# Rounding the attention's outputs in its own steps, and joining the output projection to them

## The reference

```
x = x + xattn(layernorm(x), ctx)        # cross attention and own attention, fp8 weights and activations
x = x + sparse(layernorm(x))            # top-6 sparse attention
x = x + ternary_ffn(layernorm(x))       # ternary weights, 512 -> 2048 -> 512

def xattn(h, cond):
    ln_out = ln(h)
    q, k, v, qx = [fp8_linear(ln_out, w) for w in (wq, wk, wv, wqx)]     # q, qx: 16 heads of 128, k, v: 8
    core = gqa(ln(q), ln(k), v)                                          # within 64 tokens
    kx, vx = split(cond @ w_kv_x.T); kx = ln(kx)
    xout = gqa(ln(qx), kx, vx)                                           # over 1601 context tokens
    cat  = concatenate([core, xout], axis=-1)                            # 4096 features
    catq = fp8(bfloat16(clip(cat / proj_smooth, -448, 448)))
    return (catq @ wproj.T) * (proj_in_scale * proj_w_scale)
```

## Time and profile before

| | |
|---|---|
| three runs | 2127.19, 2126.93, 2124.67 us; median 2126.93 |
| the profiled execution | 2127.17 us, its span 2125.8 us |
| busy in the span | PE 1947.5 (92%), PEld 1641.5 (77%), DVE 1159.1 (55%), ACT 939.0 (44%), POOL 686.4 (32%) |

### The profile page before, as it was taken

How to read it: one execution, slowest core, us unless ns; L and a number is a source line. 1 busy time by engine, 2 the same in 40 slices (tenths; PEclk the granted TensorE clock), 3 DMA queues, 4 the chain that set the end, 5 groups by cost and what they waited for, 6 DMA issues and landing times. The chain is left out here.

```text
span 2125.8 us, 30938 instructions
## 1 busy us (share of the span) xinstructions
PE 1947.5 (92%) x10316; PEld 1641.5 (77%) x10316; DVE 1159.1 (55%) x2883; ACT 939.0 (44%) x1771; POOL 686.4 (32%) x734
## 2 busy tenths in 40 slices
PE   3899999999999999999999999999999994858769
PEld 3678888788888888888888888888888883642457
DVE  6565455445554554455446545554555443968743
ACT  4554344445544553354435534444544334518221
POOL 3224543322233332333333333343333322411310
PEclk9999999999999999999999999999999996989869
DMA  5775343435453543354445444443444225530020
GB/s 188 201 235 175 110 155 119 147 104 153 143 180 114 165 141 120 105 164 141 137 127 177 153 128 135 143 158 111 149 146 149 84 62 186 176 101 2 2 79 20
DMA packets 228588, 280.91 MB, mean 132 GB/s; under 512 B 63752, under 2 KB 134024, under 8 KB 228432
## 3 DMA queue, kind: packets, MB, share of 16 engines
q1 hardware_dynamic: 217936, 278.09, 41.6%
q10 hardware_dynamic: 8448, 0.43, 0.2%
q0 software_dynamic: 2048, 0.43, 0.1%
HBM read 239.10 MB, written 39.22 MB: 131 GB/s over the span
## 5 line engine op out<-in xcount | busy, mean ns | idle before, releaser
L496 PE MATMUL kx_ps<-ctxT_hi,wk_hi 128*128 128x400 f32 (+1 forms) x1024 | 366.4, 358 | 16.1 <-DVE ctxT_lo L295 14.9
L498 PE MATMUL kx_ps<-ctxT_lo,wk_hi 128*128 128x400 f32 (+1 forms) x1024 | 355.9, 348 | 0.0
L579 PE MATMUL u_ps<-ctxN_hi,pt_hi 128*128 128x512 f32 (+1 forms) x832 | 342.8, 412 | 13.5 <-DVE pt_lo L799 13.5
L500 PE MATMUL kx_ps<-ctxT_hi,wk_lo 128*128 128x400 f32 (+1 forms) x1024 | 355.2, 347 | 0.0
L580 PE MATMUL u_ps<-ctxN_lo,pt_hi 128*128 128x512 f32 (+1 forms) x832 | 331.9, 399 | 0.0
L581 PE MATMUL u_ps<-ctxN_hi,pt_lo 128*128 128x512 f32 (+1 forms) x832 | 330.2, 397 | 0.0
L799 DVE TENSOR_TENSOR pt_lo<-t_ps,pt_hi 128x512 fp32r<-128x512 f32 (+1 forms) x256 | 144.5, 587 | 277.1 <-ACT pt_hi L1039 277.1
L1008 ACT ACTIVATE kx_hi<-kx_ps 128x400 fp32r<-128x400 f32 (+1 forms) x256 | 129.3, 505 | 346.2 <-PE kx_ps L500 342.8
L726 DVE TENSOR_TENSOR kx_lo<-kx_ps,kx_hi 128x400 fp32r<-128x400 f32 (+1 forms) x256 | 147.0, 574 | 219.8 <-ACT sq L1010 219.6
L1039 ACT ACTIVATE pt_hi<-t_ps 128x512 fp32r<-128x512 f32 (+1 forms) x256 | 125.3, 523 | 286.2 <-PE t_ps L564 286.2
L781 DVE CUSTOM_DVE_ANT_0 prob<-sc_ps,rstd_bc 128x400 f32<-128x400 f32 (+2 forms) x256 | 136.4, 570 | 146.3 <-PE sc_ps L552 146.3
(11 more groups left out here) (247 smaller groups left out, 3647.6 us busy)
## 6 DMA issues: line engine op xcount, KB each, us to landing
rstd_bc<-scratch_rstd SPq DMA_DIRECT2D x64, 804.0 KB, 5.9
stage<-in_ctx_t SPq DMA_DIRECT2D x96, 267.0 KB, 4.6
stage<-in_ctx_n SPq DMA_DIRECT2D x96, 256.0 KB, 6.2
wk_hi<-scratch_wk_s SPq DMA_DIRECT2D x56, 256.0 KB, 3.2
wk_lo<-scratch_wk_s SPq DMA_DIRECT2D x56, 256.0 KB, 3.7
wv_hi<-scratch_wv_s SPq DMA_DIRECT2D x56, 256.0 KB, 4.9
wv_lo<-scratch_wv_s SPq DMA_DIRECT2D x56, 256.0 KB, 5.2
scratch_own_rows<-out_sb SPq DMA_DIRECT2D x32, 256.0 KB, 3.1
```

Of the source, the lines that this page charges most:

```text
L496: PE.matmul(kx_ps[:, j % 2, 0:w], wk_hi[:, g % 2, i, :], ctxT_hi[:, i, c0:c0 + w], start=(i == 0), stop=False)
L498: PE.matmul(kx_ps[:, j % 2, 0:w], wk_hi[:, g % 2, i, :], ctxT_lo[:, i, c0:c0 + w], start=False, stop=False)
L500: mm = PE.matmul(kx_ps[:, j % 2, 0:w], wk_lo[:, g % 2, i, :], ctxT_hi[:, i, c0:c0 + w], start=False, stop=(i == C - 1))
L579: PE.matmul(u_ps[:], pt_hi[0:w, t % 2, cols], ctxN_hi[0:w, y, :], start=(y == 0), stop=False)
```

## The change

- **Rounding.** In odd steps ACT's new `scale_outputs` scales a pair's outputs (four activations 128x64, two 128x128) and takes Abs (128x512), between `prob_high(n + 1, 1)` and `keys_high(n + 3, 3)`. In even steps DVE's new `round_outputs` does the four rounding operations, 512 wide, for the pair before, between `softmax_bias(n + 1)` and `keys_low(n + 3, 0)`. SP stores a pair in three DMAs, in even steps, where there were four over both steps. `cat` then holds `catq`.
- **Projection.** `project_out` goes; a class `Projection` stands in its place. Its first round is computed by PE in step 62 and its second in step 63, eight matmuls in each of four places; six rounds follow the last step. Rounds go in the order 0, 1, 4, 5, 2, 6, 3, 7, the last two token tile by token tile, with `acc_done` after each tile. The low parts of the weight are DVE's, `catq` is loaded ready, and no barrier stands ahead.
- **Norms.** `x2` and both norms are made tile by tile (`TileNorm`), in DVE's list of `attend`. POOL then waits for the last products and clears the semaphores, 119 now, ahead of the one barrier. The sparse attention's small weights are loaded in SP's list of `attend` (`Tail.load`, 13 DMAs).
- **Linear stage.** ACT makes all three high parts in item 0; DVE's low parts go in the sets `((0,), (1, 2, 3), (), ())`.
- Smaller: two semaphores of `softmax_bias` become one; the reciprocal of the smoothing is taken ahead of the steps; SBUF is laid out anew.

```diff
@@ tensor, attention @@
+                if n >= N - 2:
+                    PE.wait_ge(kx_split, 4 * N)
+                    proj.products(n - N + 2, 0, acc[0])
                 if v:
                     output(n)
...
                     keys(n + 3, 1)
+                if n >= N - 2:
+                    proj.products(n - N + 2, 1, acc[1])
                 if k:
                     keys(n + 3, 2)
+                if n >= N - 2:
+                    PE.wait_ge(scaled, 4 * N)
+                    proj.products(n - N + 2, 2, acc[2])
...
                     keys(n + 3, 3)
+                if n >= N - 2:
+                    proj.products(n - N + 2, 3, acc[3])
+            for k in range(2, 6):
+                for t in range(4):
+                    proj.products(k, t, acc[t])
+            PE.wait_ge(proj.cat_in[1], 16 * 4)
+            PE.wait_ge(proj.low_done, 8)
+            for t in range(4):
+                proj.products(6, t, acc[t])
+                proj.products(7, t, acc[t])
@@ vector @@
+            def round_outputs(u):
+                V.wait_ge(o_sized, u + 1)
+                V.tensor_scalar(o_y[:], o_y[:], 448.0, -448.0, ALU.min, ALU.max).then_inc(o_clipped, 1)
+                V.tensor_scalar(o_grid[:], o_grid[:], 1.5 * 2.0 ** 14, 448.0 * 2.0 ** 20, ALU.max, ALU.min).then_inc(o_stepped, 1)
+                V.wait_ge(o_clipped, u + 1)
+                V.wait_ge(o_stepped, u + 1)
+                V.tensor_tensor(o_res[:], o_y[:], o_grid[:], ALU.add).then_inc(o_lifted, 1)
+                V.wait_ge(o_lifted, u + 1)
+                after(V, o_stored, 48 * u)
+                V.tensor_tensor(o_cat[:], o_res[:], o_grid[:], ALU.subtract).then_inc(o_rounded, 1)
...
-                    for c in ((0,), (1,), (2, 3), ())[t]:
+                    for c in ((0,), (1, 2, 3), (), ())[t]:
                         weights_low(n + 1, c)
...
+                if v and not odd and u > 0:
+                    round_outputs(u - 1)
                 refill(3)
                 if k:
                     keys_low(n + 3, 0)
...
+                if N - 3 <= n < N - 1:
+                    proj.low(n - N + 3)
+            round_outputs(N // 2 - 1)
+            for k in range(2, 8):
+                proj.low(k)
...
+            residual(0)
+            for t in range(4):
+                middle(t)
+                if t < 3:
+                    residual(t + 1)
+                tail.norm2.vector_apply(t, tail.xln, tail.y)
@@ scalar @@
+            def scale_outputs(u):
+                g, head = u % G_, 16 + 4 * (u % (G_ // 2))
+                A.wait_ge(o_moved, 2 * u + 2)
+                A.wait_ge(own_moved, u + 1)
...
+                for h in range(4):
+                    part = slice(64 * (h % 2), 64 * (h % 2) + 64)
+                    A.activation(o_y[:, h // 2, part], o_res[:, h // 2, part], ACTF.Copy,
+                                 scale=recip_o[:, head + h:head + h + 1])
...
+                A.activation(o_grid[:], o_y[:], ACTF.Abs, scale=2.0 ** 20).then_inc(o_sized, 1)
...
-                if n + 1 < NB and t < 3:
-                    weights_high(n + 1, t)
+                if n + 1 < NB and t == 0:
+                    for c in range(3):
+                        weights_high(n + 1, c)
...
                     prob_high(n + 1, 1)
+                if v and odd:
+                    scale_outputs(u)
                 refill(6)
                 if k:
                     keys_high(n + 3, 3)
                 refill(7)
+                if N - 3 <= n < N - 1:
+                    proj.high(n - N + 3)
...
+            for k in range(2, 8):
+                proj.high(k)
@@ gpsimd @@
+            tail.norm1.gpsimd(0)
+            for t in range(4):
+                tail.norm2.gpsimd(t)
+                if t < 3:
+                    tail.norm1.gpsimd(t + 1)
+            G.wait_ge(proj.acc_done, 4)
+            G.wait_ge(tail.d_in, 16 * 11)
+            G.wait_ge(proj.high_done, 8)
+            core.clear_stage()
@@ sync @@
+                if n == N - 3:
+                    SP.wait_ge(kx_done, 4 * N)
...
+                    for k in range(2):
+                        proj.load_weights(k)
+                        proj.load_heads(k)
+                if n == N - 1:
+                    proj.load_weights(2)
...
+                if n > 0 and not odd:
+                    store_outputs(u - 1)
...
+            proj.load_weights(3)
+            store_outputs(N // 2 - 1)
+            proj.load_heads(2)
+            proj.load_heads(3)
+            SP.wait_ge(o_moved, N)
+            tail.load()
+            for k in range(4, 8):
+                proj.load_weights(k)
+                proj.load_heads(k)
```

More of the change, by code:

```diff
@@ new lines, with __init__, place, load_weights @@
+class Projection:
+    ORDER = (0, 1, 4, 5, 2, 6, 3, 7)
+    def __init__(self, core, o_stored):
+        self.c, self.o_stored = core, o_stored
+        sem = core.sem
+        self.cat_in, self.w_in = [sem("cat_in0"), sem("cat_in1")], [sem("wp_in0"), sem("wp_in1")]
+        self.high_done, self.low_done = sem("wp_high"), sem("wp_low")
+        self.part_done, self.acc_done = sem("proj_part"), sem("proj_acc")
+    def place(self, stack):
+        core = self.c
+        self.w_raw = core.sb(stack, "wp_raw", [P, 2, 4, 512])
+        self.catq = core.sb(stack, "catq", [P, 2, 4, 512], F32R)
+        self.w_hi = core.sb(stack, "wp_hi", [P, 2, 4, 512], F32R)
+        self.w_lo = core.sb(stack, "wp_lo", [P, 2, 4, 512], F32R)
+    def load_weights(self, k):
+        SP, b = self.c.SP, self.ORDER[k]
+        after(SP, self.low_done, k - 1)
+        SP.dma_start(self.w_raw[:, k % 2, :, :],
+                     self.c.dram["wprojT"][512 * b:512 * b + 512, :].rearrange("(f d) o -> d f o", d=P)
+                     ).then_inc(self.w_in[k % 2], 16)
+    def load_heads(self, k):
+        SP, b = self.c.SP, self.ORDER[k]
+        SP.wait_ge(self.o_stored, 48 * (26 + 2 * b if b < 4 else 25 + b))
+        after(SP, self.part_done, k - 1)
+        SP.dma_start(self.catq[:, k % 2, :, :].bitcast(F32),
+                     self.c.dram["cat"][4 * b:4 * b + 4, :, :].rearrange("f d s -> d f s")).then_inc(self.cat_in[k % 2], 16)
+    def high(self, k):
+        A = self.c.ACT
+        A.wait_ge(self.w_in[k % 2], 16 * (k // 2 + 1))
+        after(A, self.part_done, k - 1)
+        A.activation(self.w_hi[:, k % 2, :, :], self.w_raw[:, k % 2, :, :], ACTF.Copy).then_inc(self.high_done, 1)
+    def low(self, k):
+        V = self.c.DVE
+        V.wait_ge(self.high_done, k + 1)
+        V.tensor_tensor(self.w_lo[:, k % 2, :, :], self.w_raw[:, k % 2, :, :], self.w_hi[:, k % 2, :, :].bitcast(F32),
+                        ALU.subtract).then_inc(self.low_done, 1)
+    def products(self, k, t, bank):
+        PE = self.c.PE
+        if t == 0:
+            PE.wait_ge(self.cat_in[k % 2], 16 * (k // 2 + 1))
+            PE.wait_ge(self.low_done, k + 1)
+        for f in range(4):
+            PE.matmul(bank, self.catq[:, k % 2, f, t * P:(t + 1) * P], self.w_hi[:, k % 2, f, :],
+                      start=(k == 0 and f == 0), stop=False)
+            mm = PE.matmul(bank, self.catq[:, k % 2, f, t * P:(t + 1) * P], self.w_lo[:, k % 2, f, :],
+                           start=False, stop=(k == 7 and f == 3))
+        if k == 7:
+            mm.then_inc(self.acc_done, 1)
+        elif t == 3:
+            mm.then_inc(self.part_done, 1)
@@ L1994, in gpsimd @@
         def gpsimd():
-            norm.gpsimd(4)
+            norm.gpsimd(2)
             G.wait_ge(x_split, 2)
```

301 lines of the change are left out of this document (141 added, 160 removed).

## The result

The changed kernel takes 2090.22 us in the median of 4 runs (2086.96 to 2092.85), the kernel before beside it 2125.80 (2124.49 to 2127.19): a ratio of **0.9832**, 95% interval 0.9815 to 0.9849. That is 35.6 us less, where 45.3 were forecast (2082, range 2068 to 2104). The profiled execution took 2089.24 us, its span 2087.9.

What follows compares the result with a forecast made beforehand. PE was taken to bound the steps (busy 706.5 of 715 us), other engines the projection. Gains of 40.3 + 6 − 1 = 45.3 us off 2127.2 gave 2082, its own range 2072 to 2092, eight in ten 2068 to 2104.

Steps and rivals of the forecast that it cites:

- Part 1: Linear stage: PE's stalls cost 14.1 us, of which a replay with the new order leaves 8.0; gain 6.
- Part 2: Steps: rounding takes ACT 1.95 and DVE 2.0 us, hidden under PE with about 1 us slack; +1 taken overall.
- bound of −5: Steps: the lower bound on their cost, 5 us gained if the freed queue loads the context earlier.
- Parts 3 and 4: Last two steps and after: products end 5.8 us later, then PE stands 6.5 us instead of 25.8 before round 2.
- Part 5: Projection's six rounds after the steps: one wait of 5.2 us before rounds 6 and 7, end at 1844.2, 39.3 earlier.
- rival C: Projection: 13 transfers ahead on SP's list make round 4's weight and catq about 14 us late; 2096, chance 0.12.
- Part 6: Norms and clears: y_d 7.6 us after the products, clears 8.7, barrier 0.4; PE starts at 1860.4, gain 40.3.
- A: Linear stage: block 4's high parts come early enough and the waits vanish, 14 us instead of 6; about 2074, chance 0.13.
- B: Steps: PE notices the rounding at batch changes (13.7 us) and beside POOL's long operations (12.6); 2108, chance 0.12.
- D: Last two steps: products of rounds 0 and 1 stand in series instead of interleaving, 6 us lost; 2088, chance 0.03.
- E: Steps: the rounding lies wholly on PE's path, 122 us on top of −45; 2204, chance 0.05.
- the 6 us of waits between 83 and 130: Linear stage: a sign that the forecast is right, PE's waits there being 6 us in sum.

Runs made afterwards that it cites:

- stores late: The kernel before, with only the stores of the attention's outputs moved to the end of each step on SP's list: 2122.43 us beside 2124.05, ratio 0.9987.
- No rounding: The changed kernel with its new rounding work in the steps shrunk to one small ACT instruction and one DVE copy: steps 1579.03 us (one trace).

## Why the prediction was right, and where it was wrong

- **Part 1, the linear stage**: forecast 6, measured 6.6, and 2.8 to 5.8 in the other traces with the new order, so that 6 is at the upper end. The mechanism is right: block 4's three low parts still came behind the rounding. The replay put its wait at 4.2 (3.26 in the trace) and block 8's at 1.7 (0.68). Block 6's was not in it; it is 0.69 in this trace and up to 3.67 in others.
- **Part 2, the rounding**: the sizes and the slack hold. ACT's seven instructions run from 1281.67 to 1283.99, 2.3 us for 1.95; DVE's four from 1249.55 to 1251.56, 2.0 for 2.0. The last squares end 0.9 us ahead of their use.

```profile
1249.55 0.28 DVE L864 TENSOR_SCALAR o_y<-o_y 128x512 bf16<-128x512 bf16 x1
1249.75 0.28 DVE L865 TENSOR_SCALAR o_grid<-o_grid 128x512 bf16<-128x512 bf16 x1
1250.14 0.69 DVE L868 TENSOR_TENSOR o_res<-o_y,o_grid 128x512 f32<-128x512 bf16 x1
1250.87 0.69 DVE L871 TENSOR_TENSOR o_cat<-o_res,o_grid 128x512 f32<-128x512 f32 x1
1251.48 0.57 DVE L753 TENSOR_TENSOR kx_lo<-kx_ps,kx_hi 128x402 fp32r<-128x402 f32 x1
```

  What failed is the sign of "I take +1" for the batch changes: the steps gained, by the traces 3 to 8 us, by the whole time of stores late 0.2 to 5. The bound of −5 named the right cause, the freed queue, and the earlier trace rows had the wait of 3.11 us for `stage`; I did not follow on SP's list what stood ahead of those loads.
- **Parts 3 and 4**: PE stopped 5.4 us later against the steps, for 5.8, and stood 6.76, for 6.5. The sum of part 4 has a slip: 1785 + 5.0 is 1790.0 and not 1790.7, a wait of 5.8; the measured 6.76 is nearer to the figure with the slip, by luck.
- **Part 5**: rounds 2 and 3 took 16.8 us, for 16.7. Then the sum had no wait before round 4, and there were 5.08 and a half clock of about 1.6 behind it. This is rival C, whose mechanism, the order of SP's list, was right, and whose price was not: it took 14 us late as 14 us lost, and the cover of rounds 2 and 3, which stands under "Against", was not taken off. Its 15 us came from bytes at 175 GB/s. The engines moved up to 393 GB/s, and it was the issue that took 15.0: the same figure by luck.
- **Part 6**: `y_d` was ready 7.8 us behind the last product, for 7.6, and the clears took 8.7. The barrier's 0.4 us was the term that failed: from the last clear to PE it was 5.8, since POOL, as the last, stood 5.3 in its drain. In the kernel before, the second barrier cost 0.4 because DVE came last at it.
- Together: 5.1 + 1.6 + 5.3 = 12.0 us short, which is the difference of 40.3 and 28.3; the other terms are off by 0.5 us or less and cancel. In the whole time 9.7 us are missing, 35.6 for 45.3. The range held since it had been made wide enough to take C whole, and not since the sum was good to 2 us: two terms at the end of the kernel were too low by 6.7 and 5.3, and a gain in the steps that was not forecast gave some of it back.
- **Rivals A, B, D and E** did not come. A would have been 14 us, against 3 to 7. No rounding leaves B and E nothing to stand on. Against D, PE stopped 5.4 us later, as products that fill gaps would make it. Of the signs named, the 6 us of waits between 83 and 130 were 4.6.

## What to carry to other kernels

Price a barrier by the engine that comes last at it, not by the one that came last before: read each engine's drain at the old barrier, and if work moves so that another engine is last, a drain like it is added. Work that an engine does "for nothing" under someone's cover, such as clearing semaphores, has to find new cover when the stage goes. On a queue that issues transfers, count both the issue time and the bytes of what stands ahead, take off what the waiting engine still has to do, and look for waits for an engine's result in front of loads that nobody needs to hold back.
